# Decay exponents of a chunked delta rule moved from TensorE to GpSimd, with reordered convolution taps, substitution rows and an identity reset by DMA

## What is computed

```python
q = _causal_dwconv(x @ Wq.T, cq_w, cq_b)     # k and v likewise
g = jax.nn.log_sigmoid(x @ Wg.T)
beta = jax.nn.sigmoid(x @ Wb.T)
k = k / jnp.clip(jnp.linalg.norm(k, axis=-1, keepdims=True), 1e-12, None)
...
Sk = jnp.einsum('bhkv,bhk->bhv', S, k_t)
delta = jnp.einsum('bhv,bhk->bhkv', v_t, k_t) - jnp.einsum('bhv,bhk->bhkv', Sk, k_t)
S = jnp.exp(g_t)[..., None, None] * S + b_t[..., None, None] * delta
o_t = jnp.einsum('bhkv,bhk->bhv', S, q_t)
```

## Time and profile before

| | us |
|---|---|
| median of 3 runs (1846.21 to 1849.15) | 1846.63 |
| profiled execution, its own time | 1854.48 |
| its span, first to last instruction | 1852.7 |
| delta phase, first tap to last state update | 69 to 1202 |
| busy over the span: PE / DVE / ACT / POOL | 1576.1 / 1201.7 / 890.0 / 863.5 |

### The profile page before, as it was taken

The page is one execution under the profiler, slowest core; times in us unless marked ns, Lnnn a source line. Parts: engine busy times, 40 slices in busy tenths (PEclk is TensorE's granted clock), DMA queues, the critical chain, the costliest instruction groups (busy, mean ns, idle before and its releaser), DMA issues. The chain is left out here.

```text
span 1852.7 us, 73957 instructions
## 1 busy us (share of the span) xinstructions
PE 1576.1 (85%) x31244; PEld 1175.0 (63%) x31244; DVE 1201.7 (65%) x3061; ACT 890.0 (48%) x2282; POOL 863.5 (47%) x1070
## 2 busy tenths in 40 slices
PE   7478999999899999999999997667888985898990
PEld 6235666666666666666666665556777874787870
DVE  1388988888889889888888886234445553222224
ACT  1276767767767767667667664100011110133333
POOL 0034444443444444434444443116655665577775
PEclk9799999999999999999999998887889997999995
DMA  6235564565555655655656554274444420499757
GB/s 269 82 83 115 114 133 114 124 128 116 123 126 114 138 113 123 135 114 113 137 114 126 111 117 99 56 240 118 140 130 133 138 80 27 110 259 248 166 88 284
DMA packets 521402, 245.45 MB, mean 132 GB/s; under 512 B 423888, under 2 KB 485968, under 8 KB 520176
## 3 DMA queue, kind: packets, MB, share of 16 engines
q1 hardware_dynamic: 368976, 200.72, 41.2%
q10 hardware_dynamic: 133632, 20.98, 6.1%
q0 software_dynamic: 18464, 19.03, 5.8%
HBM read 169.29 MB, written 71.37 MB: 130 GB/s over the span
## 5 line engine op out<-in xcount | busy, mean ns | idle before, releaser
L375 PE MATMUL delta_p_j<-delta_xt,delta_w 128*128 128x512 f32 x768 | 387.7, 628 | 30.5 <-DMA delta_xt<-in_xt 17.5
L574 DVE SCALAR_TENSOR_TENSOR delta_kq<-delta_hist,cw,delta_kq 128x512 f32<-128x512 f32 x384 | 298.6, 778 | 30.7 <-ACT delta_kq L722 23.7
L1395 POOL DMA_INDIRECT slot_tokens<-mix_tokens,mix_slot x192 | 188.5, 982 | 115.5 <-DVE mix_slot L1266 59.8
L715 ACT ACTIVATE delta_hist<-delta_p_j 128x512 f32<-128x512 f32 x192 | 114.8, 598 | 240.6 <-PE delta_p_j L375 233.4
L375 PEld LDWEIGHTS delta_p_j<-delta_xt,delta_w 128*128 128x128 f32 x768 | 132.0, 192 | 146.3 <-issue 111.8
L888 POOL TENSOR_TENSOR delta_sd<-state,eg_end 128x256 f32<-128x256 f32 x128 | 104.4, 816 | 258.2 <-DVE state L654 258.2
L1074 PE MATMUL mix_p_y<-mix_wo,mix_ot 128*128 128x256 f32 x512 | 134.3, 407 | 33.3 <-issue 15.6
L863 POOL TENSOR_SCALAR delta_n<-delta_n 128x8 f32<-128x8 f32 x64 | 15.5, 242 | 287.3 <-DVE delta_n L605 287.3
L1165 PE MATMUL mix_p_h<-mix_wo,w 128*88 128x128 f32 x1024 | 126.2, 277 | 13.5 <-ACT mix_wo L1351 10.4
L588 DVE SCALAR_TENSOR_TENSOR delta_yv<-delta_hist,cw,delta_yv 128x512 f32<-128x512 f32 x128 | 132.1, 1032 | 8.2 <-ACT delta_yv L722 5.9
L1074 PEld LDWEIGHTS mix_p_y<-mix_wo,mix_ot 128*128 128x128 f32 x512 | 99.3, 202 | 58.3 <-issue 44.9
(11 more groups left out here) (148 smaller groups left out, 3607.5 us busy)
## 6 DMA issues: line engine op xcount, KB each, us to landing
delta_xd<-x_scratch SPq DMA_DIRECT2D x256, 128.0 KB
delta_w<-in_wqkv SPq DMA_DIRECT2D x64, 416.0 KB
w<-in_w SPq DMA_DIRECT2D x64, 352.0 KB
delta_eg<-eg_rows SPq DMA_DIRECT2D x128, 130.0 KB, 3.2
n_scratch<-delta_kkq ACTq DMA_DIRECT2D x128, 128.0 KB
ot<-delta_o SPq DMA_DIRECT2D x128, 128.0 KB
mix_ot<-ot SPq DMA_DIRECT2D x16, 1024.0 KB
w<-in_w SPq DMA_DIRECT2D x64, 176.0 KB
```

The costliest lines, as they stand in the source:

```text
L375: mm = pe.matmul(p_j[:, :], w[e][:, (ch * 3 + n) * 128:(ch * 3 + n) * 128 + 128], xt[m // 8 % 2][:, ch * 512:ch * 512 + 512], start=ch == ...
L574: ve.scalar_tensor_tensor(out, view(hist[e], i * 2 * 518 + tap, (259, 2), (1, 256)), cw[:, column:column + 1], out, ALU.mult, ALU.add).the ...
L715: ac.activation(view(hist[e], n * 518 + 3, (259, 2), (1, 256)), p_j[:, :], ACT.Copy)
L1395: po.indirect_dma_start(out=s.tok.ap(), out_offset=bass.IndirectOffsetOnAxis(ap=slot[i % 2][:, k:k + 1], axis=0), in_=tokens[:, i:i + 1], ...
```

## The change

- The exponents are no longer a matmul. SP loads G of all tokens of the unit's row into a tile `span` of 128 partitions (two DMAs of 64 partitions with 2 KB each, every partition the same row). POOL subtracts the key's own G (`cum`, now kept in SBUF from the gates phase) and adds the mask of -1e30 (`C_LATER`), in two operations of 128x512 in place. ACT reads `span` where it read `p_j`.
- In POOL's queue `exponent(m)` stands in slot m, behind a wait for the query taps of macro m-1. Behind it stands a wait for all key taps of macro m, then `decay_state` of the second step.
- At the start of a slot POOL waits for the first of the two value taps of the macro before. `roots` moves ahead of `factors` and `weight`.
- The two value taps on DVE are split: tap 2 stays at the slot's end (in odd slots it goes behind the second `horner`), tap 1 goes to the start of the next slot, ahead of the query taps. In odd slots the three key taps stand together.
- The substitution is cut anew: before, 6 rows in the odd slot and 9 in the even one; now 8 and 7, and the last rows of each stand behind the first `horner`.
- `xi` is set by a DMA on SP's queue, just ahead of the load of `kb`, in place of POOL's copy.
- The loads of `arg_l` and `arg_r` in the gates phase go, with SP's wait for them.

```diff
@@ SyncE @@
                 for sh in range(2):
-                    sp.dma_start(view(arg_l[e], sh * C, (1, C), parts=(64 + sh * 8, 8)),
-                                 bass.AP(s.g_rows, m * 1024 + sh * 512, [[C, 8], [1, C]])).then_inc(r_in[e], 16)
-                sp.dma_start(view(arg_r[e], 0, (1, 512), parts=(80, 2)),
-                             bass.AP(s.g_rows, m * 1024, [[512, 2], [1, 512]])).then_inc(r_in[e], 16)
+                    sp.dma_start(span[e][64 * sh:64 * sh + 64, :],
+                                 bass.AP(s.g_rows, m * 1024 + sh * 512, [[0, C], [1, 512]])).then_inc(r_in[e], 16)
...
                 sp.wait_ge(kk_out[group % 2], 64 * (group // 2 + 1))
+                if group >= 1:
+                    sp.wait_ge(x_out[(group - 1) % 2], 16 * ((group - 1) // 2 + 1))
+                    sp.wait_ge(xit_out, group)
+                sp.dma_start(xi[:, :], a["const"][:, C_EYE:C_EYE + SUB * SUB]).then_inc(xi_set, 16)
@@ TensorE @@
-                if n == 1 and m == 0:
-                    pe.wait_ge(tap_k, 1)
-                if n == 1 and m >= 1:
-                    pe.wait_ge(exped, m)
+                if n == 1:
+                    pe.wait_ge(tap_k, m + 1)
...
-                if is_macro(before):
-                    exponents(before)
@@ VectorE, the loop over slots @@
                 if is_macro(before):
+                    conv_values(before, 1)
                     conv(before, 1, tap_q, conv_q)
                     gate(before)
...
                 if is_macro(m):
-                    conv(m, 0, tap_k, conv_k, (2,))
+                    conv(m, 0, tap_k, conv_k, (2, 1, 0) if t % 2 else (2,))
                 if two_:
                     residual(*two_)
-                if is_macro(m):
+                if is_macro(m) and t % 2 == 0:
                     conv(m, 0, tap_k, conv_k, (1, 0))
@@ ScalarE @@
-                ac.wait_ge(arg, m + 1)
+                ac.wait_ge(arg, 2 * m + 2)
...
-                ac.activation(view(ex[e], 1, (C + 1, 8), (1, C)), view(p_j, 0, (C, 8), (1, C)), ACT.Exp).then_inc(exped, 1)
+                ac.activation(view(ex[e], 1, (C + 1, 8), (1, C)), view(span[e], 0, (C, 8), (1, C)), ACT.Exp).then_inc(exped, 1)
@@ GpSimd @@
+            def exponent(m):
+                e = m % 2
+                po.wait_ge(r_in[e], 32 * (m // 2 + 1))
+                po.tensor_tensor(view(span[e], 0, (C, 8), (1, C)), view(span[e], 0, (C, 8), (1, C)),
+                                 view(s.cum, m * 8, (1, 8), (0, C)), ALU.subtract).then_inc(arg, 1)
+                po.wait_ge(arg, 2 * m + 1)
+                po.tensor_tensor(view(span[e], 0, (C, 8), (1, C)), view(span[e], 0, (C, 8), (1, C)),
+                                 view(const, C_LATER, (0, 8), (1, C)), ALU.add).then_inc(arg, 1)
...
+                if is_macro(before):
+                    po.wait_ge(conv_v, 2 * before + 1)
                 if one:
                     decay_state(*one)
...
-                if t % 2 and 0 <= (t - 3) // 2 < NG:
...
-                    po.tensor_copy(xi[:, :], const[:, C_EYE:C_EYE + SUB * SUB]).then_inc(xi_set, 1)
+                if is_macro(m):
+                    if m >= 1:
+                        po.wait_ge(conv_q, 3 * m)
+                    exponent(m)
+                    po.wait_ge(conv_k, 3 * m + 3)
                 if two_:
                     decay_state(*two_)
                 if is_macro(before):
                     clip(before)
+                    roots(before)
                     factors(before)
                     weight(before)
-                    roots(before)
```

## The result

The changed kernel takes 2025.5 us (median of 4 runs, 2013.5 to 2033.3) against 1846.4 for the kernel before: ratio 1.096, interval 1.091 to 1.102. Forecast: 1885, at most 1925. The direction was right; the cost was +179 us where I gave +39.

The account below looks back on a forecast made before the run. PE and DVE, both nearly full, hold each other up. DVE's 29.3 us a pair plus collisions and `kb` gives 35.0, 17.5 a slot against 16.70: +45, less 5 and 1, +39 on 1846.6, 1885 us; range 1840 to 1925.

Parts of the forecast that it names:

- The credit of 1.06 + 0.7 us a slot: PE per slot: exponents' matmul (1.06) and its wait for DVE's `horner` (0.7) both come off 16.55 us.
- the 14.8 us a slot: What PE needs per slot once the exponents' matmul and the `horner` wait are gone, from about 16.55.
- 1.2 us of exponents: Odd slot: late exponents run beside substitution and `lengths`, blocking DVE about 0.35 + 0.85; bounds 0.7 and 1.7.
- The law "the second waits for the first less 0.15 to 0.2": Two-SBUF-input DVE operations against GpSimd: whichever comes second waits for the first, less 0.15 to 0.2 us.
- My sum without `kb`: DVE per pair of slots: 29.3 plus exponents 1.5 and 1.2, `decay_state` 0.8, `weight` 1.1.
- my floor of 14.65: DVE's work per slot without waits for PE or blocked time, value taps split: 29.3 us a pair.
- PE then hides its own small hitches: PE at 14.8 against 17.5 a slot has slack, so the comparison uses the mean slot, 16.70, not the undisturbed pair.
- The late span: Odd slot: spans issued from 5.4 us, 1.6 for issues, 3.2 for landing, there at 9.5 to 10.
- The third rival: GpSimd's queue bounds the odd slot; the mask waits 1 us a pair, +28 more, 1913 us; chance 0.2.
- The first rival: Collisions mostly miss, beside PSUM readers or idle DVE: 16.05 a slot, -36 us; chance 0.18 with all faster ends.
- the doubt whether the exponents run where they are put: Odd slots: exponents run wherever the load lands, not behind query taps; were rows early, 1871 us; chance 0.12.
- the signs I listed: PE's share down some 10 points, state-product waits almost vanishing, DVE work up over 1 us, late odd exponents, `kb` waits.

Follow-up runs that it names:

- k_pe_light: Kernel before with the exponents' matmul cut from 512 columns to 8 and ScalarE's exp reading a constant tile; ratio 0.999 (0.996 to 1.002).
- The four pairs: Four kernels with exponents on GpSimd or those operations narrowed, each run without and with an idle TensorE matmul of the old exponents' size; ratios fell 0.8, 0.5, 0.4, 0.6 points.
- Two edits: Against the kernel before: all of the change except the exponents, which stay on TensorE, 1.006; only the exponents moved to GpSimd, old order elsewhere, 1.072.

## Why the prediction was wrong

- **What bounds the kernel.** Both engines nearly full, each holding the other up: right. That PE's 1.06 us are worth something was not: k_pe_light gives 0.999. The credit of 1.06 + 0.7 us a slot was taken from PE's sum, not from the waits it would end; in the pair of slots of the earlier trace rows these were 1.90 and 0.15, and of the first k_pe_light's odd slot still has 1.51, partly since TensorE waits for `xd` instead. Nor did PE fall to the 14.8 us a slot that I gave it: it is busy 15.99, 1.0 of the difference in the projections, some of which ran at the lower clock.
- **DVE's work.** Right in the sum, nearly exactly, with some luck in the terms. I gave every odd slot 1.2 us of exponents; there are 1.4 to 2.0 in 12 of 21 and none in the other 9. `weight` blocks 1.7 us in the pair shown, where I gave 1.1. The law "the second waits for the first less 0.15 to 0.2" holds: `gate` starts its last 1.22 us at 668.43, 0.14 before GpSimd's end at 668.57. Terms: `gate` +0.78 (forecast 0.73); the row behind it +1.06 (0.77, since the second operation takes 1.26, not 1.04); `decay_state` 0.39 in an even slot, 0.34 or nothing in an odd one (0.4). My sum without `kb` is 33.9 a pair, 16.95 a slot, of which 16.95 - (14.65 - 13.9) = 16.2 is work: before, DVE's 14.71 less 0.8 blocked is 13.9, and the rest of my floor of 14.65 was small gaps. Measured: 16.24.
- **DVE's waits: the step that failed.** The sum let DVE's waits for PE vanish, put `kb` at 0.55 and put nothing for what stands behind the late spans. That left 17.5 - 16.2 = 1.3 us of idle time in a slot; it is 3.38. That is 2.1 x 56 = 116 of the missing 140 us. The waits that the trace names add up to 2.0 of these 2.1: the reciprocal 0.84, the state products 0.49, the mask 0.31, and 0.37 more for `kb`. Most of the remaining 24 are terms of the same kind: the first five slots became 1.5 us longer each (16.4 for 14.9), +7 where I gave -5, and the slots outside the measured stretch are as long as those in it. "PE then hides its own small hitches" has no counterpart in the trace: DVE still waits 0.49 for state products and 0.31 for the mask.
- **The late span.** I forecast its landing at 9.5 to 10 and wrote that `clip`, `roots`, `factors` and `weight` "move back with them", without a price. The price was 0.84 us a slot: DVE's reciprocal stands in the middle of the slot, in front of rows that need nothing of it. The landing was late too: over 20 odd slots of the window, GpSimd started 10.9 to 13.7 after the slot's start, middle 12.3. The loads were issued at 6.8 and not 5.4, the two issues took 2.5 and not 1.6 (3.85 in the slot shown is the longest), and 2.9 passed to the start, where I gave 3.2. My own terms, 5.4 + 1.6 + 3.2, already add up to 10.2. The third rival saw GpSimd's queue but named the wrong place (the mask waiting for `weight`) and too small a price (28 us).
- **`kb` and `xd`.** `kb` 0.92 a slot against 0.55, above its upper bound (1.8 a pair, bound 1.6). PE waits for the reload of the inverse too (40.4 us in 20 pairs), which I did not follow.
- **The first rival** (collisions mostly miss) and the doubt whether the exponents run where they are put: the collisions hit, and in odd slots the exponents indeed run where the load lands. Of the signs I listed, PE's share (94% to 81%), DVE's work, `gate`, the late exponents (12.3 after the slot's start against 3.4 in even slots, 8.9 later and not 6) and the `kb` waits came true; DVE's waits for the state products fell to a third but did not almost vanish (19.9 us in 20 waits). The last one came true as well, "if slots lengthen with DVE not fuller, the waits are of another kind": DVE's share fell from 87% to 83%.
- **The clock** stood in no term. The four pairs show 0.4 to 0.8 points for the part of it that came back, net of the added work; its whole share in the changed kernel stays open.

## What to carry to other kernels

Cost a moved operation twice: by what it blocks while it runs, and by what stands behind it in its queue while it waits for its input, down to the smallest operation that another engine needs in the middle of its own queue. Before crediting the engine that gets shorter, look in one slot at what it would wait for next; a credit read from busy sums is an upper bound, and here it was worth nothing. Two edits do not add up either: alone they cost 0.6% and 7.2%, together 9.9%. I read this as slack that both draw on; no run isolates it.

## What the runs showed of the hardware

- The Trainium skill ("SBUF — State Buffer", section "Who interferes with whom") calls the port pair that a DVE operation with two SBUF inputs shares with a GpSimd operation reading SBUF "an exclusive lock". The traces agree, but for the length: the second of the two takes its own free duration counted from 0.14 to 0.2 us before the first one's end, in every collision looked at. It holds for DVE's shortest operations too: a row of 0.22 us takes 1.28.
- The two GpSimd operations of 128x512 have one shape and differ: 1.04 us with `cum` as second input, 1.26 with the mask.
- GpSimd's `roots` (pow on 8 columns) blocks nobody: value taps beside it keep 0.75. It takes 2.11 us itself beside them in the kernel before, and 1.66 in the changed one, where it stands beside substitution rows.
- With TensorE's gaps growing (busy 94% to 81% of the window) its granted clock fell from 1.00 to 0.93, with single projections at 1.2 GHz, and one idle matmul of 1.1 us a slot brought it back to 1.00 in the old order, but only to 0.95 in the changed kernel.
- The two DMA issues of G in an odd slot take 1.2 to 2.9 us before (middle 1.5; 1.59 in the earlier trace rows) and 1.8 to 3.9 after (middle 2.5), when each fills 64 partitions with 2 KB.
